# Attention inside chunks of a delta-rule scan: compact scores, one masking product, outputs in two parts

## What is computed

```python
x = x + attn(layernorm(x)); x = x + xattn(layernorm(x), ctx, ctx, mask); x = x + ffn(layernorm(x))

def step(S, inp):                      # S: (b, NH, D, D), scanned over the 512 tokens
    q_t, k_t, v_t, beta_t = inp
    retrieval = jnp.einsum('bhij,bhj->bhi', S, k_t)
    S = S + jnp.einsum('bhi,bhj->bhij', beta_t * (v_t - retrieval), k_t)
    o_t = jnp.einsum('bhij,bhj->bhi', S, q_t)
    return (S, o_t)
```

## Time and profile before

| | |
|---|---|
| median of 3 runs | 993.28 us (992.77 to 994.01) |
| the profiled execution | 988.93 us, span 987.1 us from first to last instruction |
| TensorE busy | 852.7 us, 86% |
| VectorE busy | 818.5 us, 83% |
| ScalarE busy | 672.3 us, 68% |
| GpSimd busy | 520.6 us, 53% |
| chain that ended last | PE 61%, DVE 18%, ACT 11%, issue 9% |
| recurrent stage | from some 30 us to some 635 us |

### The profile page before, as it was taken

The page is one execution under the profiler, slowest core; times in us unless marked ns, Lnnn a source line. Parts: engine busy times, 40 slices in busy tenths (PEclk is TensorE's granted clock), DMA queues, the critical chain, the costliest instruction groups (busy, mean ns, idle before and its releaser), DMA issues.

```text
span 987.1 us, 19474 instructions
## 1 busy us (share of the span) xinstructions
PE 852.7 (86%) x6225; PEld 654.2 (66%) x6225; DVE 818.5 (83%) x2448; ACT 672.3 (68%) x1693; POOL 520.6 (53%) x499
## 2 busy tenths in 40 slices
PE   7899999999999999999999999879999804993376
PEld 7677777877777777777787777556666503441254
DVE  4888888888988888888888887755777786999887
ACT  4778787786677777777767765536777741993195
POOL 6455756655466565565455654445887841960000
PEclk9999999999999999999999999999999955997599
DMA  9900000000000000004000000133110000000022
GB/s 159 157 7 7 7 9 10 6 9 10 7 7 12 6 7 12 7 7 138 8 7 9 10 6 9 43 122 129 65 65 0 2 0 1 1 1 1 1 75 97
DMA packets 28573, 30.49 MB, mean 31 GB/s; under 512 B 5549, under 2 KB 23865, under 8 KB 28473
## 3 DMA queue, kind: packets, MB, share of 16 engines
q1 hardware_dynamic: 28256, 29.12, 12.1%
q10 hardware_dynamic: 216, 0.14, 0.1%
HBM read 20.85 MB, written 4.19 MB: 25 GB/s over the span
## 4 chain that ended last, share of the span: by engine, by line
PE 61%; DVE 18%; ACT 11%; issue 9%; POOL 1%; DVEq 0%; ACTq 0%; POOLq 0%
PE ps L1963 10%; PE psY L1931 6%; PE psX L1931 6%; PE psG L1917 5%; PE ps L1955 4%; PE ps L2079 4%; ACT arena L713 3%; PE psG L1911 3%; PE psX L2100 3%; DVE arena L1389 3%; PE psY L2100 2%; PE ps L2279 2%; PE psG L1912 2%; DVE arena L1336 2%; ACT arena L722 2%
## 5 line engine op out<-in xcount | busy, mean ns | idle before, releaser
L509 POOL TENSOR_SCALAR_AFFINE_SELECT arena<-arena 128x2048 f32<-128x2048 f32 x32 | 64.4, 2013 | 174.2 <-DVE arena L1286 174.2
L524 POOL TENSOR_TENSOR work<-work,half 128x16 f32<-128x16 f32 x32 | 97.5, 3045 | 2.7
L513 POOL TENSOR_SCALAR_AFFINE_SELECT arena<-arena 128x2048 f32<-128x2048 f32 x32 | 92.1, 2878 | 2.2
L713 ACT ACTIVATE arena<-ps 128x512 f32<-128x512 f32 x128 | 69.3, 593 | 28.3 <-PE ps L1955 27.8
L1955 PE MATMUL ps<-work 32*128 32x256 f32 x512 | 81.1, 400 | 1.2 <-ACT arena L713 1.2
L1955 PEld LDWEIGHTS ps<-work 32*128 32x128 f32 x512 | 52.4, 184 | 35.1 <-issue 28.9
L1931 PE MATMUL psY<-work,arena 128*128 128x96 f32 (+1 forms) x512 | 60.1, 276 | 12.5 <-DVE arena L1389 12.5
L1305 DVE TENSOR_REDUCE arena<-arena 128x64 f32<-128x256 f32 (+1 forms) x96 | 65.9, 687 | 3.3
L1931 PEld LDWEIGHTS psY<-work,arena 128*128 128x128 f32 x512 | 58.4, 192 | 15.2 <-DVE arena L1389 15.2
L1931 PE MATMUL psX<-work,arena 128*128 128x96 f32 (+1 forms) x480 | 56.3, 276 | 10.4 <-DVE arena L1389 10.4
L1931 PEld LDWEIGHTS psX<-work,arena 128*128 128x128 f32 x480 | 54.7, 192 | 12.8 <-DVE arena L1389 12.8
(11 more groups left out here) (348 smaller groups left out, 2486.5 us busy)
## 6 DMA issues: line engine op xcount, KB each, us to landing
arena<-in_mask_BxSxS_ik SPq DMA_DIRECT2D x8, 1024.0 KB, 6.9
xs<-arena SPq DMA_DIRECT2D x256, 16.0 KB, 1.8
arena<-in_ctx SPq DMA_DIRECT2D x8, 512.0 KB, 4.6
out<-xs SPq DMA_DIRECT2D x32, 128.0 KB, 1.7
arena<-in_x SPq DMA_DIRECT2D x8, 288.0 KB, 19.1
arena<-in_L_ffn_w SPq DMA_DIRECT2D x2, 1024.0 KB, 24.4
arena<-in_x SPq DMA_DIRECT2D x16, 96.0 KB, 7.0
arena<-in_L_attn_w_qkvb SPq DMA_DIRECT2D x2, 512.0 KB, 4.7
```

Source lines behind the costliest of these rows:

```text
L509: G.affine_select(out=keys, in_=keys, compare_op=ALU.is_ge, fill=0.0, base=0, pattern=[[0, NH], [1, P]], channel_multiplier=-1).then_inc(h ...
L513: G.affine_select(out=pairs, in_=pairs, compare_op=ALU.is_ge, fill=0.0, base=0, pattern=[[0, NH], [-CT, B], [0, CT]], channel_multiplier=1 ...
L524: own(G.tensor_tensor(root, length, half, ALU.pow))
L713: A.activation(attn[j % 2][:, r * 512:(r + 1) * 512], ps[(2, 0)[r % 2]][:, :], ACT.Copy).then_inc(att_out, 1)
```

## The change

Scores are computed only inside the two halves of 64 rows (four batches each), since a batch never reaches across. `attention(j, part)` for part 0 and 1 makes, for each half u of the rows, a product of 32 key rows by 64 columns with the queries of the same half. The scores then fill 16 x 64 columns; ScalarE copies two banks instead of four, and GpSimd masks them with one product with `same_half`, a mask of 64 columns built once at the start (which adds operations ahead of `consts`). `outputs(j, u)` runs once for each half, with 64 rows instead of 128 and 64 moving columns, and `norms_turned` stands between the two. Attention part 0 stands ahead of the far gram.

Beside that: the expansion of the state is split into the first 8 and the last 8 heads on ScalarE and, in the same way, on VectorE (four calls of 32 x 256 instead of two of 32 x 512), and `retrieval` waits for each half by itself. `updates_turned` moves ahead of the retrieval on TensorE, into bank ps2, with `updates_out` first on ScalarE and the copy to `ust` right behind the state. In the tail `gq` has three buffers, the products go round four banks, and VectorE clamps six tiles ahead.

```diff
+        def down_bank(n):
+            return (psX, psY, ps[0], ps[1])[n % 4][:, 0:D]
+        def update_bank(j):
+            return ps[2] if j < NCK - 1 else ps[0]
         def flat(ap):
...
                 G.memset(g3[:, :, t, 2 + t], 1.0).then_inc(consts, 1)
+            G.memset(all_pairs, 1.0).then_inc(half_masked, 1)
+            pool.wait_ge(half_masked, 1)
+            G.affine_select(out=all_pairs, in_=all_pairs, compare_op=ALU.is_ge, fill=0.0, base=0,
+                            pattern=[[1, P]], channel_multiplier=-1).then_inc(half_masked, 1)
+            pool.wait_ge(half_masked, 2)
+            blocks = all_pairs.rearrange("p (b t) -> p b t", t=CT)
+            G.affine_select(out=blocks, in_=blocks, compare_op=ALU.is_ge, fill=0.0, base=0,
+                            pattern=[[-CT, B], [0, CT]], channel_multiplier=1).then_inc(half_masked, 1)
+            pool.wait_ge(half_masked, 3)
+            for u in range(2):
+                rows = slice(HALF * u, HALF * u + HALF)
+                G.tensor_copy(same_half[rows, :], all_pairs[rows, HALF * u:HALF * u + HALF]).then_inc(half_masked, 1)
+            pool.wait_ge(half_masked, 5)
+            G.memset(all_pairs, 0.0).then_inc(consts, 1)
             def mask_attention(j):
-                pool.wait_ge(att_out, 4 * (j + 1))
-                keys = attn[j % 2].rearrange("p (h t) -> p h t", h=NH)
-                G.affine_select(out=keys, in_=keys, compare_op=ALU.is_ge, fill=0.0, base=0,
-                                pattern=[[0, NH], [1, P]], channel_multiplier=-1).then_inc(half_masked, 1)
-                pool.wait_ge(half_masked, j + 1)
-                pairs = attn[j % 2].rearrange("p (h b t) -> p h b t", h=NH, t=CT)
-                G.affine_select(out=pairs, in_=pairs, compare_op=ALU.is_ge, fill=0.0, base=0,
-                                pattern=[[0, NH], [-CT, B], [0, CT]], channel_multiplier=1).then_inc(att_masked, 1)
+                pool.wait_ge(att_out, 2 * (j + 1))
+                keys = attn[j % 2][:, 0:NH * HALF].rearrange("p (h t) -> p h t", h=NH)
+                G.tensor_tensor(keys, keys, same_half.rearrange("p (a t) -> p a t", a=1).broadcast_to([P, NH, HALF]),
+                                ALU.mult).then_inc(att_masked, 1)
             own = Chain(pool, pool_chain)
...
                 act.wait_ge(s_mm, j)
-                for r in range(2, 4):
-                    rows = slice(32 * r, 32 * r + 32)
-                    for e in range(2):
-                        cols = slice(32 * r + HD * e, 32 * r + HD * e + HD)
-                        last = A.activation(sexp[rows, :, cols],
-                                            psS[rows, :].rearrange("p (h n) -> p h n", n=32)[:, :, HD * e:HD * e + HD],
-                                            ACT.Copy, scale=nparity[rows, e:e + 1])
-                last.then_inc(sexp_act, 1)
+                for heads in (slice(0, NH // 2), slice(NH // 2, NH)):
+                    for r in range(2, 4):
+                        rows = slice(32 * r, 32 * r + 32)
+                        for e in range(2):
+                            cols = slice(32 * r + HD * e, 32 * r + HD * e + HD)
+                            last = A.activation(sexp[rows, heads, cols],
+                                                psS[rows, :].rearrange("p (h n) -> p h n", n=32)[:, heads, HD * e:HD * e + HD],
+                                                ACT.Copy, scale=nparity[rows, e:e + 1])
+                    last.then_inc(sexp_act, 1)
...
                 last.then_inc(kexp_ready, 1)
-            def attention_out(j, r):
-                act.wait_ge(att_mm, 4 * j + r + 1)
-                if r == 0 and j >= 1:
+            def attention_out(j, f):
+                act.wait_ge(att_mm, 2 * j + 2)
+                if f == 0 and j >= 1:
                     act.wait_ge(o_mm, j - 1)
...
             for j in range(NCK + 1):
                 m = j + 3
+                if exists(j - 1):
+                    updates_out(j - 1)
                 if j >= 1 and exists(j + 1):
                     key_copied_out(j + 1)
                 if j >= 1 and exists(j):
                     state(j)
                 if exists(j - 1):
-                    updates_out(j - 1)
+                    updates_turned(j - 1)
                 if exists(j):
                     queries_by_parity(j)
                 if j >= 1 and exists(j + 3):
                     scaled_by_feature(j + 3)
                 if exists(j) and j < NCK - 1:
                     keys_spread(j)
-                if exists(j - 1):
-                    updates_turned(j - 1)
                 if j >= 1 and exists(j + 2):
                     key_sums_out(j + 2)
...
             def updates_turned(j):
                 pe.wait_ge(upd_out, j + 1)
-                pe.wait_ge(att_out, 4 * (j + 1))
-                pe.wait_ge(beta_ready, min(j + 4, NCK))
-                pe.wait_ge(nT_ready, min(j + 5, NCK))
+                pe.wait_ge(att_out, 2 * (j + 1))
+                pe.wait_ge(mixed_out, j)
                 for f in range(DC):
-                    last = M.transpose(ps[0][:, f * P:(f + 1) * P], upd[:, f * P:(f + 1) * P], ident[:, :])
+                    last = M.transpose(update_bank(j)[:, f * P:(f + 1) * P], upd[:, f * P:(f + 1) * P], ident[:, :])
                 last.then_inc(uT_mm, 1)
...
             def retrieval(m):
-                pe.wait_ge(sexp_dve, m)
-                pe.wait_ge(sexp_act, m)
                 pe.wait_ge(k_ready, m + 1)
                 pe.wait_ge(dq_ready, m + 1)
                 first = 2 * (m % 4)
                 rows = padded[:, first:first + 3, :].rearrange("p z (k h t) -> p h z k t", k=2, t=CT)
                 into = psR[m % 2][:, :].rearrange("p (h k t) -> p h k t", k=2, t=CT)
                 for h in range(NH):
+                    if h % (NH // 2) == 0:
+                        pe.wait_ge(sexp_dve, 2 * m - 1 + h // (NH // 2))
+                        pe.wait_ge(sexp_act, 2 * m - 1 + h // (NH // 2))
                     a, b = 1 if h == 0 else 0, 2 if h == NH - 1 else 3
                     last = M.matmul(into[:, h - 1 + a:h - 1 + b], sexp[:, h, :], rows[:, h, a:b],
                                     start=False, stop=True, skip_group_check=True)
...
-            def attention(j, r):
-                if r == 0:
+            def attention(j, part):
+                if part == 0:
                     pe.wait_ge(qe_ready, j + 1)
-                    if j >= 1:
-                        pe.wait_ge(mixed_out, j - 1)
-                elif r == 1:
                     pe.wait_ge(ust_ready, j)
+                    pe.wait_ge(nT_ready, min(j + 4, NCK))
                 else:
-                    pe.wait_ge(att_out, 4 * j + r - 1)
-                rows = slice(32 * r, 32 * r + 32)
+                    pe.wait_ge(att_mm, 2 * j + 1)
                 for f in range(DC):
-                    last = M.matmul(ps[(2, 0)[r % 2]][:, f * 2 * P:(f + 1) * 2 * P], kq[j % 4][rows, f * P:(f + 1) * P],
-                                    qe[rows, f].rearrange("p e t -> p (e t)"), start=True, stop=True)
+                    for u in range(2):
+                        tokens = slice(HALF * u, HALF * u + HALF)
+                        for r in (2 * part, 2 * part + 1):
+                            rows = slice(32 * r, 32 * r + 32)
+                            first = part * 2 * P + f * P
+                            last = M.matmul(ps[(2, 0)[r % 2]][tokens, first:first + P].rearrange("p (e t) -> p e t", e=2),
+                                            kq[j % 4][rows, f * P + HALF * u:f * P + HALF * u + HALF],
+                                            qe[rows, f, :, tokens], start=True, stop=True)
                 last.then_inc(att_mm, 1)
...
-            def outputs(j):
-                pe.wait_ge(ust_ready, j + 1)
-                pe.wait_ge(att_masked, j + 1)
+            def outputs(j, u):
+                if u == 0:
+                    pe.wait_ge(ust_ready, j + 1)
+                    pe.wait_ge(att_masked, j + 1)
+                else:
+                    pe.wait_ge(first_out, j + 1)
                 into = psR[j % 2][:, :].rearrange("p (f b k t) -> p f k b t", f=DC, k=2, t=CT)
+                rows = slice(HALF * u, HALF * u + HALF)
                 for f in range(DC):
                     for e in range(2):
                         for r in range(4):
-                            at_ = r * 512 + (2 * f + e) * P
+                            at_ = r % 2 * 512 + r // 2 * 2 * P + f * P + e * HALF
                             cols = slice(f * P + 32 * r, f * P + 32 * r + 32)
-                            last = M.matmul(into[32 * r:32 * r + 32, f, 1], ust[:, e, cols],
-                                            attn[j % 2][:, at_:at_ + P].rearrange("p (b t) -> p b t", t=CT),
+                            last = M.matmul(into[32 * r:32 * r + 32, f, 1, 4 * u:4 * u + 4], ust[rows, e, cols],
```

(38 more changed lines are left out.)

46 lines of the change are left out of this document (26 added, 20 removed).

## The result

The changed kernel takes 999.93 us (median of 6 runs, 998.58 to 1003.39) beside 993.16 of the kernel before on the same chip: 1.0076 of before, 95% interval 1.0054 to 1.0098. It is slower by 0.8%, against a forecast of 972.6. Its profiled span is 997.9, 10.8 longer than before. Each experiment further down was run side by side with the kernel before, whose median in those rounds lay between 989.2 and 993.5; the ratios say more than differences between the times of two rounds.

The account below looks back on a forecast made before the run. The recurrence was taken to bound: 30 periods falling from 18.81 to 18.24 us save 16.8, and with first chunk 1.0, end of stage 0.9 and tail 2.0 that is 20.7: 993.28 becomes 972.6, range 966 to 986.

Parts of the forecast that it names:

- The norms afterwards: Norms' chain through ScalarE, GpSimd and TensorE each chunk: TensorE waits 1.0 us for the norms, chain 18.1, just under 18.24.
- A: Rival, as forecast: the recurrence bounds at about 18.24 us a chunk, 968 to 977 us; chance 55%.
- B: Rival: the norms or ScalarE take over as bound, period 18.4 to 18.7, 979 us, range 976 to 986; chance 27%.
- D: Rival: small tiles on TensorE run one after another, period 21.3, giving 1064 us; chance 9%.
- E: Rival: GpSimd's mask product locks VectorE out, delaying the solver's transposes, 30 x 2.3 slower, about 1058 us; chance 3%.
- Blocks of small tiles, 0.60 each: Attention and outputs blocks on TensorE: 0.60 us each (bounds to 1.07 and 1.01), four taking 2.4 against 3.35 before.
- Retrieval 1.37 after the state matmuls: Split expansion lets the retrieval start 1.37 us after the state matmuls instead of 1.78; ScalarE's short calls 0.28 each.
- The recurrence at 18.24, and 0.15 a chunk without the split: Loop of retrieval, solver, state matmuls and expansion: 18.65 before, 18.24 after; unless it is shortened, only 0.15 a chunk is gained.
- Product and constants at nothing: GpSimd's mask product (0.73 to 2.9 us) and start constants (1.5 us) hide in idle time or waits, costing nothing.
- First chunk, -1.0: Queries wait less for ScalarE's copies and the first retrieval gains 0.4: 1.0 us saved, bounds 0 and 2.
- End of the stage, -0.9: After the last retrieval of the recurrent stage, waits for score copies fall away: 0.9 us saved, bounds 0 and 2.
- Tail, -2.0: Third buffer, four banks and six tiles of lead remove ScalarE and VectorE waits: 2.0 us saved, bounds 0 and 3.

Follow-up runs that it names:

- gap_filled: Changed kernel with four useless full-tile matmuls put into TensorE's wait ahead of the norms' turning in every chunk; 972.19 us, 0.9816 of before.
- norms_last: Changed kernel with the norms' turning moved back behind both outputs blocks, no work added; 972.78 us, 0.9844 of before.
- outputs_full_rows: Changed kernel with each outputs block multiplying all 128 rows instead of its half's 64, attention's part of the result wrong; 973.61 us, 0.9823 of before.
- split_undone: Changed kernel with the norms' turning behind both outputs blocks and the state's expansion in one piece again; 990.76 us, 1.0004 of before.
- start_mended: Changed kernel with norms' turning behind both outputs blocks; in the first chunk, far gram ahead of attention and dummy matmuls in two waits; 965.85 us, 0.9756 of before.
- half_rows_alone: Kernel before with its 16 outputs matmuls multiplying only rows 0 to 63, no wait added ahead of the norms; 993.57 us, 1.0027 of before.
- sums_first: Changed kernel with ScalarE copying the key sums ahead of spreading the keys instead of behind it; 977.77 us, 0.9873 of before.
- gap_small_tiles: Changed kernel with the wait ahead of the norms' turning filled by 24 small-tile matmuls of 64 rows by 32 columns; 974.50 us, 0.9872 of before.
- tail_alone: Kernel before with only the changed kernel's tail: third buffer for quantised tiles, four PSUM regions, six tiles of lead; 988.42 us, 0.9958 of before.

## Why the prediction was wrong

**The step that failed** is "TensorE ... waits 1.0" in *The norms afterwards*, together with the blocks' price. The wait was foreseen, at its place and in its size (28.1 us in 29 times, 0.97 each), and was costed as time that the recurrence hides. All matmuls around it were costed at full clock without saying so.

The runs showed that the wait, with outputs tiles that fill half of the array on both sides of it, brings TensorE's clock to half in 16 of the 29 chunks behind the first, 1.65 us each: 26.4 us. The last period adds 1.05. Together that is about the 27.4 between the spans of `gap_filled` (970.5) and of the changed kernel (997.9); `norms_last` (970.0) and `outputs_full_rows` (972.1) are as far away. The first two fill or shorten the wait, the third widens the tiles, and each comes out at the time that was forecast (972 to 974). That these two together do it is shown by frequency: beside full rows the clock fell in 0 and in 1 of 29 chunks, beside half rows in 16 of 29 and in 27 of 27. Why half rows do it is not shown, nor what picks the chunks.

None of the rivals named it: A and B assume a clock that holds, D and E are slower by another mechanism. (The chances for slower, 9% and 3%, make 0.12 and not 0.11.)

**Blocks of small tiles, 0.60 each.** Right: the attention blocks are 0.60 apart from what follows them (401.81 to 402.41), the outputs blocks 0.58 in the chain. So the switch costs what the trace of before had shown, and rival D is out. What the blocks do to the clock was not in the price.

**Retrieval 1.37 after the state matmuls.** Right: they end at 413.76 by the chain and the retrieval starts at 415.15, 1.39 later. ScalarE's short calls take some 0.31 instead of 0.28.

```profile
413.78 2.49 ACT L702 ACTIVATE arena<-ps,nparity 32x128 f32<-32x128 f32 x8 [0.51 <-PE ps L1917]
...
414.69 0.38 PE L1927 MATMUL ps<-ident,work 128*128 128x128 f32 x2
...
415.15 3.76 PE L1955 MATMUL psX<-work,arena 128*128 128x64 f32 x32
```

**The recurrence at 18.24, and 0.15 a chunk without the split.** Right: 18.28 in `norms_last`, where it bounds visibly, and 18.73 in `split_undone` (sum: 18.65). So without the split all of the smaller work on TensorE, ScalarE and GpSimd is worth 0.08 a chunk (18.81 less 18.73).

**The norms at 18.1.** 0.2 too low: turned 12.9 after the end of keys instead of 12.65, since ScalarE's expansion ends later. In the changed kernel the norms' chain bounds, in `norms_last` the recurrence, both at 18.28.

**Product and constants at nothing.** The product takes 2.36 (bounds 0.73 and 2.9), and GpSimd is idle for 3.26 ahead of it; rival E did not come.

**First chunk, -1.0.** Wrong, it was +1.7, and the first period is 1.1 longer as well (19.92, before 18.84); start and first period differ by a few us between executions, as said below. The forecast saw the copies that fall away and missed two things. Attention part 0 now stands ahead of the far gram and waits for ScalarE, and the far gram runs behind it at half clock: 3.63 instead of the 1.88 that it takes in the kernel before.

```profile
32.66 0.67 PE L1981 MATMUL ps<-work 32*64 32x128 f32 x16 [1.84 <-ACT arena L791]
33.26 3.63 PE L1940 MATMUL psG<-arena 128*128 128x512 f32 x4
```

`start_mended` gives it back and more. How much of its 3.4 us at the first retrieval is the order and how much the dummies was not tried.

**End of the stage, -0.9.** Right: from the last retrieval to ScalarE's first work on the second scale 317.7 (before 318.6). **Tail, -2.0.** Nearly right: 53.2 from there to the end (before 55.9), so 2.7 less. Four tiles take 5.11 (forecast 5.2 to 5.3). By itself the last addition comes 4.7 sooner, but the last stores then take 5.1 instead of 3.1, so 2.0 of it goes to the output's transfer.

## What to carry to other kernels

A wait that is "hidden" because another loop is as long is only free while TensorE's granted clock holds; here it cost 27 us. Before a change that makes blocks short and small-tiled and leaves TensorE waiting beside them, look at the granted clock in narrow windows afterwards, not at the busy share, and look for periods that take turns. The cheap cures are to close the wait by order (`norms_last`) or to put useless matmuls in it. In `outputs_full_rows` full rows cured it too, but as built it adds up scores that don't belong there, so it shows the cause and is no cure as it stands. And where periods are nearly all equal before (18.81 to 18.84 in 24 of 30 here), print them all after: the mean (19.25) would have looked like a new bound.

## What the runs showed of the hardware

TensorE's granted clock fell to half behind a wait of 1.0 us in a chunk of 18 to 20, with TensorE otherwise busy nearly all the time, and how often it fell went by the tiles around the wait. Behind the first chunk, with outputs matmuls of 64 by 32 it fell in 16 of 29 chunks (wait of 1.01) and in all of 27 (1.28). With 128 by 32, in the same time and number, it fell in none (1.02) and in one (1.28). In the wait's absence 64 by 32 did nothing (`half_rows_alone`). Shorter waits beside 64 by 32 were not always free: with 0.43 (`sums_first`) one period is 19.63, with 0.35 (`gap_small_tiles`) one is 19.95. The Trainium skill, "TensorE: Matmul & The Clock Gate", section "A second HAM failure mode: psum-queue depth-cycling", says that a TensorE that idles for short moments between groups of matmuls often enough swings between its two clock levels. The trace agrees on the swing; that the tiles' rows take part in it is what these runs add. The same page, "Architectural detail: the array is 16× 32×32, not 1× 128×128", describes the array as sub-arrays of 32 by 32. That fits tiles of 64 by 32, four side by side, using half of them; that the clock goes by this share is my reading and not shown, since the runs changed only rows, and only those of the outputs, while the attention tiles fill half in every one of them.

A stretch of lower clock in the first chunk came and went between profiled executions: the first period is 18.84 in the profile of before and 20.47 in `tail_alone`, whose code is the same there. It is 21.95 in `half_rows_alone`, where the low clock (0.50) begins at about 48, ahead of the first retrieval and so of the outputs matmuls that this run changed. Runs of before lie between 988 and 995. `start_mended`, whose first chunk has no such wait, has all five runs within 965.1 and 967.4.
